# A graph network kernel: a table pass with four PSUM banks, and e_r and the loop term made in ranked order

## The reference, cut to what matters

```python
for l in range(3):
    ht = einsum('nd,rdo->nro', h, W_rel[l])                  # 16 relations
    h_rel = segment_sum(ht[src, etype], dst, n)
    h_rel = h_rel + h @ W_loop[l] + b_rel[l]                 # "loop term"
    z = (h @ W_gat[l]).reshape(n, 4, 32)
    el = sum(z * attn_l[l], -1);  er = sum(z * attn_r[l], -1)
    e = leaky_relu(el[src] + er[dst], 0.2)
    ex = exp(e - segment_max(e, dst)[dst])
    alpha = ex / segment_sum(ex, dst)[dst]
    h_gat = segment_sum(alpha[:, :, None] * z[src], dst).reshape(n, 128) + b_gat[l]
    hc = concatenate([h_rel, h_gat], 1) @ W_fuse + b_fuse
    if l == 0:
        hc = hc * sigmoid(concatenate([hc, mean(edge_weight)], 1) @ W_gate + b_gate)
    h = relu(hc)
return layernorm(x + h)
```

## Time and profile before

| | us |
|---|---|
| median of three runs | 3614.19 |
| the profiled execution's own time | 3614.48 |
| its span, first to last instruction | 3612.8 |
| POOL busy | 2538.0 (70%) |
| DVE busy | 2410.2 (67%) |
| PE busy | 667.1 (18%) |
| ACT busy | 425.1 (12%) |
| POOL's first table gather begins | 234.09 |

### The profile page before, as it was taken

The page is one execution under the profiler, slowest core; times in us unless marked ns, Lnnn a source line. Parts: engine busy times, 40 slices in busy tenths (PEclk is TensorE's granted clock), DMA queues, the critical chain, the costliest instruction groups (busy, mean ns, idle before and its releaser), DMA issues.

```text
span 3612.8 us, 19127 instructions
## 1 busy us (share of the span) xinstructions
PE 667.1 (18%) x1822; PEld 354.8 (10%) x1822; DVE 2410.2 (67%) x3234; ACT 425.1 (12%) x819; POOL 2538.0 (70%) x2691
## 2 busy tenths in 40 slices
PE   6931111122222230111111221221000000000000
PEld 4510000011111110000000100110000000000000
DVE  6616666777667764676667656663777777867776
ACT  3630111111111120011111111111000000000000
POOL 1257777777777747777777777774777777777774
PEclk8975555555555565555555565555555555555555
DMA  6785544445554545444445544554533343333332
GB/s 225 302 305 106 151 147 131 150 150 159 164 150 149 172 144 112 128 150 146 137 146 158 164 150 150 171 148 136 106 105 105 105 105 104 104 105 105 103 104 58
DMA packets 149846, 516.04 MB, mean 143 GB/s; under 512 B 45477, under 2 KB 52442, under 8 KB 137026
## 3 DMA queue, kind: packets, MB, share of 16 engines
q0 software_dynamic: 132768, 452.67, 44.2%
q1 hardware_dynamic: 17058, 63.15, 4.6%
HBM read 349.48 MB, written 166.20 MB: 143 GB/s over the span
## 4 chain that ended last, share of the span: by engine, by line
POOL 43%; issue 31%; DVE 11%; DMA 6%; PE 4%; POOLq 3%; DVEq 1%; SPq 1%; ACT 0%; ACTq 0%
POOL meta_nat L587 17%; POOL late L587 15%; POOL scratch L587 10%; DVE acc L1336 3%; DMA scratch<-table,stage_tail 2%; DVE scratch L1332 1%; DMA late<-table,stage_mid 1%; PE ps_table L877 1%; DVE late L1332 1%; POOL table L666 1%; PE ps_cnt L910 1%; POOLq L357 1%; DVE meta_nat L1332 1%; DMA meta_nat<-table,stage_head 1%; DMA table<-rows 1%
## 5 line engine op out<-in xcount | busy, mean ns | idle before, releaser
L587 POOL DMA_INDIRECT meta_nat<-table,stage_head x1200 | 1139.3, 949 | 403.1 <-issue 371.3
L587 POOL DMA_INDIRECT late<-table,stage_mid x768 | 729.2, 949 | 234.2 <-issue 231.1
L587 POOL DMA_INDIRECT scratch<-table,stage_tail x558 | 529.9, 950 | 173.0 <-issue 173.0
L1000 PE MATMUL ps_mix<-ident,hr 128*128 128x128 f32 x75 | 35.3, 471 | 2125.6 <-DVE hg L1355 2125.6
L779 ACT ACTIVATE ps_cnt<-logit 128x68 f32<-128x68 f32 x192 | 44.7, 233 | 2947.3 <-DVE logit L1318 2947.3
L1336 DVE TENSOR_REDUCE acc<-meta_nat 128x132 f32<-128x2112 f32 x75 | 290.6, 3875 | 7.7
L1326 DVE TENSOR_REDUCE acc<-meta_nat 128x128 f32<-128x2048 f32 x75 | 282.5, 3767 | 0.0
L1024 PE MATMUL ps_table<-wrel,hT 128*128 128x512 f32 x400 | 264.1, 822 | 0.0
L1308 DVE TENSOR_TENSOR raw<-late,er_cur 128x64 f32<-128x64 f32 x48 | 12.8, 267 | 375.5 <-DMA late<-table,stage_mid 375.5
L1000 PEld LDWEIGHTS ps_mix<-ident,hr 128*128 128x128 f32 x75 | 13.6, 181 | 2174.8 <-DVE hg L1355 2174.8
L1308 DVE TENSOR_TENSOR raw<-meta_nat,er_cur 128x64 f32<-128x64 f32 x75 | 20.0, 267 | 291.8 <-DMA meta_nat<-table,stage_head 289.2
(11 more groups left out here) (194 smaller groups left out, 1732.2 us busy)
## 6 DMA issues: line engine op xcount, KB each, us to landing
table<-rows SPq DMA_DIRECT2D x50, 1040.0 KB, 5.2
meta_nat<-table,stage_head POOLq DMA_INDIRECT x1200, 2.8
late<-table,stage_mid POOLq DMA_INDIRECT x768, 2.8
scratch<-table,stage_tail POOLq DMA_INDIRECT x558, 2.8
meta<-meta_ranked SPq DMA_DIRECT2D x1, 3956.0 KB, 20.1
wrel<-in_L_gnn_W_rel POOLq DMA_DIRECT2D x2, 1024.0 KB, 13.8
meta_nat<-in_x SPq DMA_DIRECT2D x1, 832.0 KB
table<-rows,stage_id POOLq DMA_INDIRECT x50, 7.9
```

What stands on the lines that cost most here:

```text
L587: pool.indirect_dma_start(out=slots[b][:, k, :], out_offset=None, in_=table[l % 2], in_offset=bass.IndirectOffsetOnAxis(ap=index, axis=0)) ...
L1000: pe.transpose(mix[0], hr[:], ident[:])
```

## The change

- **Table pass.** A tile's four chunks go to four PSUM banks. ACT moves two banks with one instruction (128 x 1024), and writes z and e_l with one (128 x 2112). Each buffer of `rows` is saved by one DMA of 2.08 MB, and ACT refills it when that has landed. `z_product` has 132 columns.
- **e_r and the loop term of layer 0** are no longer made for natural tiles. When `meta` is loaded and the table pass is over, a loop over 25 ranked tiles makes them: PE transposes x of the ranked tile and multiplies it by the 132 columns, ACT copies twice a tile. DVE waits for tile t's e_r at the start of tile t of layer 0.
- **Scatters** carry start, degree, id, x and list: 212 numbers, not 344, and the load into `meta` too. They don't wait for e_r.
- **Waits for x.** Each of the three later pieces has its own semaphore, and PE waits for a piece before the first transpose of a tile in it.
- **POOL's loads.** `edge_rows` is written ahead of the loads of biases and of the weights of layers 1 and 2, so these now come after DVE's L1119.
- **DVE.** The mask of the lists is made (in bf16) before the class counts are waited for, `tw_mean` too; after the ranks the lists are masked first, and the largest degrees after them.

The diff, cut:

```diff
-            load_x(2, ROUNDS, s_xload)
+            load_x(2, ROUNDS, s_xload[0])
...
-            load_x(ROUNDS, T - 1, s_xload)
+            load_x(ROUNDS, T - 1, s_xload[1])
...
             def save_rows(t, k):
                 to = table[0][bass.ds(t * (P * R), P * R), :].rearrange("(p r) f -> p (r f)", r=R)
-                sp.reg_add(n_rows, n_rows, 1)
-                sp.wait_ge(s_half, n_rows)
-                sp.dma_start(to[:, 0:half], rows_k[:, 0:half]).then_inc(s_saved[k][0], 16)
-                sp.reg_add(n_both, n_rows, 1)
-                sp.wait_ge(s_rows, n_both)
-                sp.dma_start(to[:, half:2 * half], rows_k[:, half:2 * half]).then_inc(s_saved[k][1], 16)
+                sp.wait_ge(s_rows, n_rows)
+                sp.reg_add(n_rows, n_rows, 1)
+                sp.dma_start(to, rows[k][:].rearrange("p r f -> p (r f)")).then_inc(s_saved[k], 16)
...
-            sp.dma_start(meta[:, 0:2, :], by_rank[:, 0:2, :]).then_inc(s_meta_first, 16)
-            sp.dma_start(meta[:, 2:T, :], by_rank[:, 2:T, :]).then_inc(s_meta, 16)
+            sp.dma_start(meta[:, 0:2, 0:SCATTERED], by_rank[:, 0:2, :]).then_inc(s_meta_first, 16)
+            sp.dma_start(meta[:, 2:T, 0:SCATTERED], by_rank[:, 2:T, :]).then_inc(s_meta, 16)
...
+            pool.wait_ge(s_edge_rows, 1)
+            pool.dma_start(edge_rows[0:E, :].rearrange("(p c) o -> p (c o)", p=EP), src_i[:]
+                           ).then_inc(s_edge_saved, 16)
             pool.dma_start(wfuse[:], W_fuse.rearrange("(k d) o -> d k o", k=2)).then_inc(s_bload, 16)
...
-            pool.wait_ge(s_edge_rows, 1)
-            pool.dma_start(edge_rows[0:E, :].rearrange("(p c) o -> p (c o)", p=EP), src_i[:]
-                           ).then_inc(s_edge_saved, 16)
...
-                pool.wait_ge(s_er, t + 1)
                 pool.indirect_dma_start(
                     out=meta_ranked[:], out_offset=bass.IndirectOffsetOnAxis(ap=rank_u[:, t:t + 1], axis=0),
...
+            def natural_tile(k, next_x=True):
+                act.wait_ge(s_saved[k], n_saved[k])
                 act.reg_add(n_saved[k], n_saved[k], 16)
+                evacuate_half(k, 0).then_inc(s_bank, 1)
+                act.wait_ge(s_z_ps, n_tab)
+                s.activation(rows[k][:, :, D:ROW], bc(ps_z[:, 0:D + H], R), ACT.Copy)
+                if next_x:
+                    transposed_x(1 - k)
+                evacuate_half(k, 1).then_inc(s_rows, 1)
...
+            act.wait_ge(s_meta_first, 16)
+            act.wait_ge(s_meta, 16)
+            transposed_x(1)
+            for t in range(T):
+                if t < T - 1:
+                    transposed_x(t % 2)
+                act.wait_ge(s_er_ps, t + 1)
+                s.activation(meta[:, t, M_ER:META], ps_er[t % 2], ACT.Copy).then_inc(s_er, 1)
...
             def transpose_x(t, k):
+                if t in X_PIECES[1:]:
+                    pe.wait_ge(s_xload[X_PIECES.index(t) - 1], 16)
...
             def first_half(t, k, next_x=True):
                 pe.wait_ge(s_hT[k], n_hT[k])
                 pe.reg_add(n_hT[k], n_hT[k], 1)
-                chunk(k, 0)
-                z_product(0, k, ZW)
-                chunk(k, 1)
+                pe.wait_ge(s_bank, n_tab)
+                products(k, 0)
+                z_product(0, k, D + H)
...
-            pe.wait_ge(s_xload, 48)
             for t in range(1, ROUNDS):
                 round_(t, t % 2)
...
+            step(v.tensor_tensor(ell_valid, bc(iota_slot[:], T), bc_last(degree[:], ELL), ALU.is_lt))
             dve.wait_ge(s_cls_ps, 1)
...
+            def start_tile(l, t):
+                if l == 0:
+                    dve.wait_ge(s_er, n_t)
                 v.tensor_copy(er_cur[:], meta[:, bass.ds(t, 1), M_ER:M_LOOP]).then_inc(s_tile, 1)
```

More of the change, by code:

```diff
@@ L234, in gnn_kernel @@
         ps_table = ps("ps_table", [P, 2048])
-        ps_tab = [ps_table[:, 512 * i:512 * i + 512] for i in range(2)]
-        ps_rel = ps_table[:, 1024:1536]
-        ps_gat = ps_table[:, 1536:2048]
         ps_mix = ps("ps_mix", [P, 512])
@@ L714, in _ @@
                 if l == 0:
-                    for k, j in ((0, 0), (0, 1), (1, 0), (1, 1)):
-                        pool.wait_ge(s_saved[k][j], 16 * (T // 2 + 2 - k))
+                    for k in range(2):
+                        pool.wait_ge(s_saved[k], 16 * (T // 2 + 2 - k))
                 else:
@@ L844, in _ @@
             for k in range(2):
-                for j in range(2):
-                    act.wait_ge(s_saved[k][j], 16 * (T // 2 + 2 - k))
-            act.wait_ge(s_meta_first, 16)
-            act.wait_ge(s_meta, 16)
+                act.wait_ge(s_saved[k], 16 * (T // 2 + 2 - k))
             n_last = counter(act, "act_last_tile", 0)
@@ L889, in second_half @@
             def second_half(k):
-                chunk(k, 2)
-                chunk(k, 3)
+                products(k, 1)
                 pe.reg_add(n_tab, n_tab, 1)
@@ L971, in _ @@
                 tiles = range(4 * c, min(4 * c + 4, T))
-                place = (ps_rel, ps_gat)[c % 2][:, 0:len(tiles) * CLS].rearrange("p (t v) -> p t v", v=CLS)
+                place = (ps_place, ps_cnt)[c % 2][:, 0:len(tiles) * CLS].rearrange("p (t v) -> p t v", v=CLS)
                 pe.wait_ge(s_diag, c + 1)
@@ L990, in _, with transpose_ranked @@
                 natural_tile(t, t % 2, next_x=t < T - 1)
+            def transpose_ranked(t, k):
+                pe.transpose(mix[k], meta[:, t, M_X:M_ELL], ident[:]).then_inc(s_xT_ps, 1)
+            pe.wait_ge(s_meta_first, 16)
+            pe.wait_ge(s_rows, T + 1)
+            transpose_ranked(0, 1)
+            pe.wait_ge(s_meta, 16)
+            for t in range(T):
+                k = (t + 1) % 2
+                pe.wait_ge(s_hT[k], n_hT[k])
+                pe.reg_add(n_hT[k], n_hT[k], 1)
+                if t < T - 1:
+                    transpose_ranked(t + 1, 1 - k)
+                if t > 1:
+                    pe.wait_ge(s_er, t - 1)
+                pe.matmul(ps_er[t % 2], hT[k][:], wz[:, 0, D + H:ZW], start=True, stop=True).then_inc(s_er_ps, 1)
+            pe.wait_ge(s_er, T)
             pe.wait_ge(s_bload, 16 * (5 + 3 * L))
```

139 lines of the change are left out of this document (60 added, 79 removed).

## The result

The changed kernel took **3594.8 us** (median of 4 runs, 3589.67 to 3595.81), against 3616.26 us before (4 runs, 3613.04 to 3621.26): a ratio of 0.9936, 95% interval 0.9921 to 0.9951, so it is faster by 21.5 us. The prediction was 3595.5. The profiled execution took 3589.67 (span 3588.1), the quickest of the four.

A forecast was written before the change was run, and what follows sets the result against it. POOL's gathers were taken to bound the layers, and the table pass their first gather. 17.1 us at the start and 1.7 between histogram and first gather made 18.8, from 3614.48 to 3595.7, median 3595.5; range 3584 to 3608.

The forecast's parts named there:

- It passes on one for one: Layers run at POOL's gather pace, so whatever moves the first gather (234.09 us before) moves the end as much.
- Whatever the other engines do: From the first gather on, the layers last as POOL's gathers set, with 0.3 us idle of its own ahead of each.
- The start: Up to the histogram's copy: separate waits for x and moved weight loads bring it to 111.1 from 128.2, 17.1 us earlier.
- the first save's issue: SP's issue of save 0 in the table pass: at 36.0 instead of 40.30, ends 31 and 40.3.
- The landing: Save 0 of `rows`, from issue to landing: 9.5 us, ends 7.9 and 11.6, so landed at 45.5.
- Histogram to scatter: DVE's lists after the histogram: first scatter at H + 43.9 = 155.0, scatters ending at 187, a leg that no longer counts.
- The table pass: Tiles 16 to 24: one interval at 6.1 us, five at 7.0, two at 6.1; saved at 213.4, first gather at 215.3.
- The loop: Ranked tiles: 25 steps of 1.2 us from 220 to 250; costs nothing unless over 39 us late.
- More is gained: Rival: save 0 issued at 32 and intervals of 5.8 us, 11.6 us more gained, 3584 us; chance 0.12.
- Slower: Rival: two whole-tile buffers give 13 us an interval, first gather at 280, 3660 us; from 9.1 us an interval; chance 0.05.
- Nothing is passed on: Rival: `meta`, lists or loop hold the first tiles and the layers wait longer, about 3612 us; chance 0.11.
- The prediction's own sign of being wrong: Wrong if tiles stand 9 us apart, PE's second stop lasts beyond 55, or POOL waits for DVE in tile 1.

The follow-up runs named there:

- chip C: Third chip of the follow-ups, kernel before 3613.35 us; changed kernel with no gather before the ranked loop has ended: 3617.42 us, ratio 1.0012.
- chip B: Second chip of the follow-ups, kernel before 4102.21 us; changed kernel with each scatter waiting for its natural tile's table rows: 4083.33 us, ratio 0.9967.
- The third buffer: Changed kernel with constants in ACT's ranked loop and a third buffer for `rows` over `meta`'s unused part: 3583.47 us, ratio 0.9918 to the kernel before.
- the doubled and the fivefold loop: Changed kernel with the ranked loop run twice and five times, DVE waiting for its end: 4115.69 us (1.0028) and 4163.85 us (1.0144).
- chip A: First chip of the follow-ups, kernel before 4135.92 us; the changed kernel, unedited, took 4117.31 us there, ratio 0.9957.

## Why the prediction was right

**The frame.** "It passes on one for one" held: 25.2 us and 24.7, and again with 34.1 and 35.3 on chip C. "Whatever the other engines do" was too strong: POOL waits some 82 us for ACT and DVE at stores and at the output. These waits stayed, as shown above.

**The start, right in kind and too small.** Histogram forecast at 111.1, measured 106.12. The term that was mis-sized is the first save's issue, 36.0 against 29.95. I had taken q1's rate in 36:43, 0.101 MB/us, as its most. It moved 0.157 MB/us at 59.7% of the engines, where 36:43 had 29.6%: that window showed what happened to be in the queue then, and was no bound. The trace of the kernel before had the answer, in 30:36, when POOL's loads were over (packets, MB, share):

```profile
...
q1 hardware_dynamic: 1307, 1.11, 85.3%
...
```

That is 0.185 MB/us. The end that I gave for the issue, 31, was itself too late. The landing made up for a part: 11.2 us (29.95 to the start of ACT's move at 41.17) instead of 9.5, close to my end of 11.6. So tile 3's products began at 44.31 and not 48.7. From there to the histogram I had 62.4 and got 61.8.

The landing itself came out longer than the 9.5 us. The Trainium skill's rule that a copy of 125 partitions runs on 5 engines ("DMA: Bandwidth & Descriptors", "Why a DMA increments its semaphore by 16 and not by 1") was held to support a longer landing. The trace agrees as far as it goes: q1's share in 30:32, behind the save's issue, is 27.0%, near 5 of 16. But SP issued the second save at 33.3, into the same queue, before the first had landed, and from 34 the engines are full. No run here took the edge arrays or that save away, so the cause of the 11.2 us is not shown.

**Histogram to scatter.** Forecast 43.9, measured 43.35. No run took DVE's new order away. The scatters ended at 181.85 instead of 187 and waited for nobody, and the leg was slack, as said; with the waits put back (chip B) it was the last leg again, by 2.2 us.

**The table pass.** 6.5 us an interval, forecast 6.66, and the start of tile 16 at H + 37.8, forecast 36.4 (H is the histogram's time). With the last landing and `meta` behind it, the first gather came 102.8 us after the histogram, forecast 104.2. The working of it was a turn of two buffers, 6.1, and 7.0 beside scatters; three of the nine starts waited for PE instead. The third buffer showed that the turn hides another limit: with it the DMA engines take its place, and the first gather is 2.7 us earlier. The two limits lie so near each other that a sum by either one gives nearly the same, and in that the 6.66 was lucky.

**The loop.** 0.8 us a step, within the bounds of 0.6 to 2, ended 27 us after the first gather, forecast 35. That it costs nothing here is shown by POOL's first gather of tile 1, which follows the first gather of all by 72.7 us as before and waits 0.30 us; put ahead of the gathers, the loop costs 27 to 30. The limit was forecast at 39 us of lateness, which is 62 us after the first gather; the doubled and the fivefold loop give 59.

**The sum.** First gather 208.89 instead of 215.3, so 6.4 us more was gained than forecast, 5.0 of it by the histogram. The profiled execution, on which the sum was made, was forecast at 3595.7 and took 3589.67. The median over runs lies 5 us above that one, since the quickest of the four was profiled, and so within 0.7 us of the forecast. By medians the gain is 21.5 us, by the two traces 24.7; the forecast had 18.8. The closeness of the median is luck; the error of the working is 6 us, and it lies mostly in the first save's issue, 6 us too late, against which the landing, 1.7 too short, made up a part. Two slips stand in the working beside the sum: with 6.9 us for a save in place of 7.9, the last landing would be 1.0 shorter too, so the sum 2.5 better and not 1.5; and intervals of 5.8 are 0.86 below the 6.66 each, not 0.95.

**The rivals.** "More is gained" had it right for the start (a save at 32), and wrong for intervals of 5.8. "Slower" by intervals over 9.1 did not come: none was over 8.7. "Nothing is passed on" does not hold on the first chip and on C, but a part of it does on chip A: there POOL waited 25.6 us behind the loop, and from the first gather to the end the changed kernel took 3889.6 us against 3876.0 in the kernel before with own semaphores. The prediction's own sign of being wrong, POOL waiting for DVE in tile 1, shows on chips A and B and not on the other two.

**Open.** Why chips A and B take 500 us more, and why the steps of ACT's loop are slow beside gathers there: chip C, where this was to be tested, does not show it. How much the four banks and the ranked e_r are worth on the first chip, by themselves, is open too; the trace shows 3.1 us behind the histogram for them, the narrower scatters and DVE's order together.

## What to carry to other kernels

When the longest leg is gathers at their own pace, find their first one, and price every edit by what it moves that one. A transfer that nobody waits for still holds those behind it and beside it: moving 2 MB of late weights out of the start was worth 8.9 us at the histogram, as much as the separate waits for x (7.9), since it freed the queue and the engine that issues. And take a queue's rate from a stretch in which it moves the same kind of transfer, and from more than one: here q1 moved 0.10 MB/us in one and 0.185 in another of the same trace.

## What the runs showed of the hardware

- Chips differ: the kernel before took 3616, 4136, 4102 and 3613 us. In the changed kernel the durations of gathers on POOL are alike (948 ns on chip A, 949 on the first); what grows is idle time: the rows "issue" of POOL's three groups of gathers are 572.2, 394.3 and 234.1 us on chip A and 398.2, 172.7 and 231.3 on the first.
- The issue of one load of 26.5 KB held SP for 8.8 to 10.8 us in every trace, whether it began at 18.8 or at 30.3 us. In the eleven with POOL's loads moved it ended between 29.1 and 30.5, and in the other three between 39.2 and 39.9. What it waits for is not shown.
- Two stops in series share the gain: own semaphores for the pieces of x alone took 8.7 us off (4127.26 against 4135.92 us, not surely a change), the rest of the change without them 8.9 (4126.99), both together 18.6.
- With both queues filled, the DMA engines moved as many packets of one as of the other, 390 and 391 in 16 us, though the bytes were 0.88 and 5.84 MB (third buffer, chip C).
